# A new slot table for two mixture-of-experts feed-forward layers around a top-k attention, and inputs loaded ahead of weights

## The reference

```python
x = x + 0.5 * ffn(layernorm(x))
x = x + attn(layernorm(x))
x = x + 0.5 * ffn(layernorm(x))
```

## Time and profile before

| | |
|---|---|
| median of 3 runs | 4933.38 us (4929.45 to 4933.44) |
| profiled execution, its own time | 4933.91 us |
| its span | 4932.1 us |
| busy: PE | 4021.6 us (82%) |
| busy: DVE | 4550.9 us (92%) |
| busy: ACT | 3383.9 us (69%) |
| busy: POOL | 3711.1 us (75%) |
| DMA, mean | 47 GB/s |

### The profile page before, as it was taken

The page is one execution under the profiler, slowest core; times in us unless marked ns, Lnnn a source line. Parts: engine busy times, 40 slices in busy tenths (PEclk is TensorE's granted clock), DMA queues, the critical chain, the costliest instruction groups (busy, mean ns, idle before and its releaser), DMA issues.

```text
span 4932.1 us, 111636 instructions
## 1 busy us (share of the span) xinstructions
PE 4021.6 (82%) x29004; PEld 3308.1 (67%) x29004; DVE 4550.9 (92%) x10838; ACT 3383.9 (69%) x8261; POOL 3711.1 (75%) x5070
## 2 busy tenths in 40 slices
PE   5767888888888888888888988888888888877667
PEld 4555766776777667676776767777677677765556
DVE  0199999999999999999999999999999999999990
ACT  2366777777777777777777777777777777766662
POOL 4456788878878787878878787888878788865554
PEclk8887999999999999999999999999999999998778
DMA  2201111111111111111111111111111111111011
GB/s 83 51 20 33 47 50 49 52 48 47 53 46 53 48 51 48 51 50 49 51 46 53 48 50 48 49 51 48 51 48 53 47 52 48 50 38 27 20 28 49
DMA packets 243181, 232.19 MB, mean 47 GB/s; under 512 B 27075, under 2 KB 176580, under 8 KB 242244
## 3 DMA queue, kind: packets, MB, share of 16 engines
q1 hardware_dynamic: 242500, 224.49, 16.5%
HBM read 214.98 MB, written 9.44 MB: 46 GB/s over the span
## 4 chain that ended last, share of the span: by engine, by line
issue 37%; POOL 30%; PE 17%; DVE 10%; ACT 3%; DVEq 1%; POOLq 1%; SPq 1%; ACTq 0%; DMA 0%
POOL HS L899 13%; DVE M L802 6%; PE pQ L490 6%; POOL S L940 6%; POOL mixT L917 4%; DVE W L804 3%; PE pFa L434 2%; PE pFa L438 2%; PE pST L474 1%; PE pST L507 1%; PE pFb L458 1%; PE pFa L378 1%; PE pO L531 1%; DVEq L240 1%; PE pFa L380 1%
## 5 line engine op out<-in xcount | busy, mean ns | idle before, releaser
L490 PE MATMUL pQ<-wf_sb,HS 128*128 128x192 f32 x8192 | 1679.8, 366 | 475.0 <-POOL HS L899 473.7
L802 DVE MAX8 M<-W 128x8 f32<-128x512 f32 x3072 | 1953.4, 675 | 0.0
L490 PEld LDWEIGHTS pQ<-wf_sb,HS 128*128 128x128 f32 x8192 | 1545.1, 216 | 556.5 <-POOL HS L899 431.3
L804 DVE MATCH_REPLACE8 W<-M,W 128x512 f32<-128x512 f32 x2048 | 1363.0, 670 | 0.0
L940 POOL TENSOR_TENSOR S<-S,RL 128x512 f32<-128x512 f32 x1024 | 1306.4, 1277 | 0.0
L706 ACT ACTIVATE RL<-S,NBI 128x512 f32<-128x512 f32 x1024 | 762.4, 745 | 388.9 <-POOL S L940 387.4
L935 POOL TENSOR_TENSOR NBI<-M,edge 128x4 f32<-128x4 f32 x512 | 102.1, 199 | 881.1 <-DVE M L802 850.7
L711 ACT ACTIVATE S<-S,NBI 128x512 f32<-128x512 f32 x1024 | 748.4, 731 | 2.1 <-POOL S L940 2.1
L695 ACT COPY S<-pST 128x512 f32<-128x512 f32 x1024 | 525.2, 600 | 242.7 <-PE pST L474 242.7
L804 DVE MATCH_REPLACE8 W<-M,S 128x512 f32<-128x512 f32 x1024 | 681.5, 670 | 0.0
L802 DVE MAX8 M<-S 128x8 f32<-128x512 f32 x1024 | 648.6, 672 | 29.5 <-issue 28.7
(11 more groups left out here) (219 smaller groups left out, 5477.9 us busy)
## 6 DMA issues: line engine op xcount, KB each, us to landing
RB<-rows_b SPq DMA_DIRECT2D x384, 256.0 KB, 3.2
RB<-rows_a SPq DMA_DIRECT2D x384, 256.0 KB, 3.3
x_b<-in_x SPq DMA_DIRECT2D x64, 128.0 KB, 2.8
out_y<-y SPq DMA_DIRECT2D x64, 128.0 KB, 1.7
wf_sb<-in_wf SPq DMA_DIRECT2D x1, 3072.0 KB, 10.4
wof_sb<-in_wof SPq DMA_DIRECT2D x1, 1024.0 KB, 12.4
rows_b<-rwT_b SPq DMA_DIRECT2D x64, 8.0 KB, 1.3
rows_a<-rwT_a SPq DMA_DIRECT2D x64, 8.0 KB, 1.3
```

Source lines behind the costliest of these rows:

```text
L490: mm = nc.tensor.matmul(pQ[:, 0:QKV], HS[:, k % 2, e, i, :], wf_sb[:, i, at:at + QKV], start=k + e + i == 0, stop=(k, e, i) == (3, 3, 1))
L802: nc.vector.max(m, src[i]).then_inc(s_tk, 1)
L804: nc.vector.match_replace(W[:, i, :], m, src[i], -BIG).then_inc(s_tk, 1)
```

## The change

- All constants of the attention's steps but `TR`, `PTE`, `PV`, `CTT` and `CTX` move. `TOP` goes from even to odd slots.
- Both tables `AT` are new. The gates of job a (`rw_st` to `hs`) are 14 slots ahead of their first use in place of 3, those of job b 11 in place of 4; `rows` is four deep for that. `ctx_rec` of a goes from 37 to 32, `ctx_norm` from 39 to 32, `y` from 87 to 95. In job b, modulo 16, `x_rstd` goes from 3 to 15 and `h` from 4 to 15, `shift` from 8 to 2, `top` from 9 to 2, `repl` from 11 to 3 and `gate` from 14 to 4.
- The projections alternate between the banks of a and b (`PBANK`). The values V0, V1 now come behind the first scores, and the move of V to its place waits for them.
- SP loads all four tiles of x of the first batch, then `wf` in four parts with a semaphore each, then the biases. Everything else of the weights (`late_loads`) comes behind the second `RB` of tile 0.
- The wait for the halved `wof_sb` goes from PE's first chunk to its first `y`; ACT's scaling is in the slot of the first `hs`.

```diff
-SC, EV, TOP, NBIAS, REL, SUB, EXP, TR, PTE, PV, CT, CTT, CTX = 2, 3, 4, 6, 7, 8, 9, 16, 17, 18, 19, 20, 21
+SC, EV, TOP, NBIAS, REL, SUB, EXP, TR, PTE, PV, CT, CTT, CTX = 3, 4, 5, 7, 9, 9, 13, 16, 17, 18, 20, 20, 21
...
 AT = {
-    "a": {k: v - 2 * TILE for k, v in {
-        "ctx_rec": 69, "ctx_norm": 71, "ctxT": 72, "x": 74, "x_mean": 75, "x_sq": 76, "x_rstd": 77, "h": 78,
-        "hT": 79, "h_rinv": 79, "lg": 81, "shift": 82, "top": 83, "pair": 84, "repl": 85, "gate": 87,
-        "gate_exp": 88, "gate_em": 89, "gate_sum": 90, "rw": 91, "rwT": 92, "rw_st": 93, "hs": 96, "qkv": 104,
-        "qkT": 105, "sc": 107, "sc_max": 107, "sc_nmax": 109, "sc_exp": 110, "sc_rec": 111, "sc_norm": 112,
-        "pT": 114, "rb2": 110, "attT": 116, "mix": 117, "y": 119, "out": 120,
-    }.items()},
-    "b": {k: v - SPAN for k, v in {
-        "x_ld": -51, "x_sum": -48, "x_mean": -47, "x_sq": -46, "x_rstd": -45, "h": -44, "hT": -43, "h_rinv": -43,
-        "lg": -41, "shift": -40, "top": -39, "pair": -38, "repl": -37, "gate": -34, "gate_exp": -33,
-        "gate_em": -32, "gate_sum": -31, "rw": -30, "rwT": -29, "rw_st": -28, "hs": -24, "qkv": -16, "qkT": -15,
-        "sc": -14, "sc_max": -13, "sc_nmax": -11, "sc_exp": -10, "sc_rec": -9, "sc_norm": -8, "pT": -6,
-        "rb2": -10, "attT": -4, "mix": -3, "y": 0, "y_mean": 2, "y_sq": 3, "y_rstd": 4, "y_norm": 5, "xn": 8,
+    "a": {
+        "ctx_rec": 32, "ctx_norm": 32, "ctxT": 33, "x": 36, "x_mean": 36, "x_sq": 37, "x_rstd": 37, "h": 39,
+        "hT": 40, "h_rinv": 40, "lg": 41, "shift": 42, "top": 42, "pair": 43, "repl": 44, "gate": 45,
+        "gate_exp": 46, "gate_em": 47, "gate_sum": 49, "rw": 49, "rwT": 50, "rw_st": 50, "hs": 64, "qkv": 72,
+        "qkT": 74, "sc": 75, "sc_max": 76, "sc_nmax": 78, "sc_exp": 79, "sc_rec": 80, "sc_norm": 81, "rb2": 81,
+        "pT": 83, "attT": 85, "mix": 88, "y": 95, "out": 98,
+    },
+    "b": {k: v - 2 * SPAN for k, v in {
+        "x_ld": 10, "x_sum": 10, "x_mean": 12, "x_sq": 14, "x_rstd": 15, "h": 15, "hT": 16, "h_rinv": 16, "lg": 17,
+        "shift": 18, "top": 18, "pair": 19, "repl": 19, "gate": 20, "gate_exp": 21, "gate_em": 23, "gate_sum": 24,
+        "rw": 25, "rwT": 26, "rw_st": 29, "hs": 40, "qkv": 48, "qkT": 50, "sc": 51, "sc_max": 51, "sc_nmax": 53,
+        "sc_exp": 55, "sc_rec": 57, "sc_norm": 57, "rb2": 57, "pT": 59, "attT": 61, "mix": 64, "y": 69,
+        "y_mean": 70, "y_sq": 71, "y_rstd": 71, "y_norm": 75, "xn": 76,
     }.items()},
 }
 
-PROJ = {"Q0": 57 - SPAN, "K0": 59 - SPAN, "V0": 61 - SPAN, "V1": 62 - SPAN, "Q1": 68 - SPAN, "K1": 70 - SPAN}
-VMOVE = 7
+PBANK = {"Q0": "b", "K0": "a", "V0": "b", "V1": "a", "Q1": "b", "K1": "a"}
+PROJ = {"Q0": -2, "K0": 0, "V0": 6, "V1": 7, "Q1": 9, "K1": 6}
+VMOVE = 8
...
 FILLS = {
-    "a": {k: (AT["a"][k], TILE, TILES) for k in ("ctxT", "x", "hT", "lg", "rwT", "qkT", "sc", "pT", "attT", "y")},
+    "a": {k: (AT["a"][k], TILE, TILES) for k in ("ctxT", "x", "hT", "lg", "rwT", "qkT", "sc", "pT", "attT", "y")}
+    | {k: (s, SPAN, NB) for k, s in PROJ.items() if PBANK[k] == "a"},
     "b": {k: (AT["b"][k], TILE, TILES) for k in ("hT", "lg", "rwT", "qkT", "sc", "pT", "attT", "y", "xn")}
-    | {k: (s, SPAN, NB) for k, s in PROJ.items()},
+    | {k: (s, SPAN, NB) for k, s in PROJ.items() if PBANK[k] == "b"},
 }
...
-                self.rows = nc.dram_tensor(f"rows_{n}", (2, E, P), F32, kind="Internal").ap()
+                self.rows = nc.dram_tensor(f"rows_{n}", (TPB, E, P), F32, kind="Internal").ap()
...
-            def early_loads():
-                sp.dma_start(wf_sb[:], wf).then_inc(s_ld_wf, 16)
+            for t in range(TPB):
+                sp.dma_start(b.x[:, t, :], x_t[t]).then_inc(s_ld_x[t], 16)
+            for k in range(4):
+                part = slice(4 * k * QKV, 4 * (k + 1) * QKV)
+                sp.dma_start(wf_sb[:, :, part], wf[:, :, part]).then_inc(s_ld_wf[k], 16)
+            sp.wait_ge(s_ini, 1)
+            for c in range(2):
+                sp.dma_start(bias[:, c, 0, :], bqk[2 * c]).then_inc(s_ld_att, 16)
+                sp.dma_start(bias[HD:P, c, 1, :], bqk[2 * c + 1, 0:P - HD, :]).then_inc(s_ld_att, 16)
+
+            def late_loads():
                 sp.dma_start(wof_sb[:], wof).then_inc(s_ld_wof, 16)
                 for g in range(GROUPS):
...
                     t, c = at
                     if not (isinstance(t, int) and t < TPB):
                         held(sp, q["read"], fill("b", w, j + J.at["y"] - J.at["x_ld"] - SPAN) + 1)
-                    held(sp, q["x_in"], t * 16)
-                    sp.dma_start(J.x[:, c % TPB, :], x_t[ds(t, 1)].rearrange("a p d -> (a p) d")).then_inc(q["x_in"], 16)
-                    if isinstance(t, int) and t == 0:
-                        early_loads()
+                        held(sp, q["x_in"], 16 * t - 16 * TPB)
+                        sp.dma_start(J.x[:, c % TPB, :], x_t[ds(t, 1)].rearrange("a p d -> (a p) d")).then_inc(q["x_in"], 16)
...
                 if at := tile(J, "rw_st", w, j):
                     t, c = at
                     held(sp, q["read"], fill(J.n, w, j + J.at["rwT"] - J.at["rw_st"]) + 1)
-                    if not (isinstance(t, int) and t < 2):
-                        held(sp, s_mix, earlier(w, j + J.at["mix"] - J.at["rw_st"] - 2 * TILE, MIXES.values()) + 1)
-                    sp.dma_start(J.rows[c % 2], J.rwT[:]).then_inc(q["rw_st"], 16)
+                    if not (isinstance(t, int) and t < TPB):
+                        held(sp, s_mix, earlier(w, j + J.at["mix"] - J.at["rw_st"] - SPAN, MIXES.values()) + 1)
+                    sp.dma_start(J.rows[c % TPB], J.rwT[:]).then_inc(q["rw_st"], 16)
                 for k in range(4):
                     if at := tile(J, "hs", w, j, 3 - 2 * k):
                         t, c = at
                         held(sp, q["rw_st"], 16 * t + 16)
                         held(sp, s_hs, chunk_no(w, j + 3) - 1)
                         sp.dma_start(RB[:, k % 2, :, :].rearrange("p e t -> p (e t)"),
-                                     J.rows[c % 2, 4 * k:4 * k + 4, :].rearrange("e t -> (e t)").partition_broadcast(P)
+                                     J.rows[c % TPB, 4 * k:4 * k + 4, :].rearrange("e t -> (e t)").partition_broadcast(P)
                                      ).then_inc(s_rb[k % 2], 16)
+                        if k == 1 and isinstance(t, int) and (J.n, t) == ("b", 0):
+                            late_loads()
...
                 if at := tile(J, "y", w, j, 1):
                     t, c = at
+                    if isinstance(t, int) and (J.n, t) == ("b", 0):
+                        pe.wait_ge(s_half, 1)
...
-                q, F = jobs["b"].sem, jobs["b"].F
                 for c in range(2):
                     for i, key in enumerate((f"Q{c}", f"K{c}")):
                         if not at_proj(key, w, j):
                             continue
-                        wait(pe, q["read"], fill("b", w, j))
+                        J = jobs[PBANK[key]]
+                        wait(pe, J.sem["read"], fill(J.n, w, j))
                         for k in range(KC):
-                            mm = nc.tensor.matmul(F[:], wqk_sb[:, i * KC + k, c * P:(c + 1) * P], xnT[:, k, :],
+                            mm = nc.tensor.matmul(J.F[:], wqk_sb[:, i * KC + k, c * P:(c + 1) * P], xnT[:, k, :],
                                                   start=k == 0, stop=k == KC - 1)
-                        mm.then_inc(q["full"], 1)
+                        mm.then_inc(J.sem["full"], 1)
...
-                        if k == 0 and isinstance(t, int) and t == 0:
-                            pe.wait_ge(s_ld_wf, 16)
-                            pe.wait_ge(s_half, 1)
+                        if isinstance(t, int) and (J.n, t) == ("b", 0):
+                            pe.wait_ge(s_ld_wf[k], 16)
...
-                        key = "K0" if c % QUADS == 0 else "K1"
-                        sl = PROJ[key] - SC - (c % QUADS) * 4 + j
-                        pe.wait_ge(jobs["b"].sem["read"], fill("b", w, sl) + 1)
+                        for key in ("Q0", "K0") if c % QUADS == 0 else ("Q1", "K1"):
+                            J = jobs[PBANK[key]]
+                            sl = PROJ[key] - SC - (c % QUADS) * 4 + j
+                            pe.wait_ge(J.sem["read"], fill(J.n, w, sl) + 1)
...
                 if J.n == "b" and (at := tile(J, "x_sum", w, j)):
                     t, c = at
-                    act.wait_ge(q["x_in"], 16 * t + 16)
+                    if isinstance(t, int) and t < TPB:
+                        act.wait_ge(s_ld_x[t], 16)
+                    else:
+                        act.wait_ge(q["x_in"], 16 * t - 16 * TPB + 16)
...
-                if (w.lo, j) == (FIRST, 20):
+                if (w.lo, j) == divmod(AT["b"]["hs"], SPAN):
...
                     if due(w, j, VMOVE + 4 * g, SPAN, NB):
+                        for key in ("V0", "V1") if g == 0 else ():
+                            J = jobs[PBANK[key]]
```

(34 more changed lines are left out.)

7 lines of the change are left out of this document (4 added, 3 removed).

## The result

The changed kernel takes 5427.29 us (median of four runs, 5411.77 to 5434.53), the kernel before 4932.78: a ratio of 1.0999, 95% interval 1.0985 to 1.1012. It is 10% slower. The prediction said slower with 0.90 and 5292 us in a range of 5115 to 5500, so the sign and the range held and the point lies 135 us too low.

The account below looks back on a forecast made before the run. DVE was taken to bound the middle, which could only grow by its waits. Start 206, middle 4566 plus 404 of waits and end 115 gave a span of 5291, forecast 5292 us, range 5115 to 5500.

Parts of the forecast that it names:

- What bounds: In the middle DVE is busy 4537.3 of 4566 us; it can only get longer, if DVE must wait.
- First wait: DVE at `ctx_rec`, end of block 15, waits for ACT's `ctxr`: 3.1 us in 55 tiles, +171 us.
- upper bound: At `ctx_rec`, a wait of 4.5 us if PE's transposes hold up ACT's copies of PTs.
- Second wait: DVE at `top` of b waits for POOL's `shift`: 4.4 us, 52 times in full, +233 us in all.
- Third place: POOL's `gate` of b waits for `repl`; 23.6 us of work fit 26.2 before `shift` of a: no wait.
- more waits: Rival: DVE waits at `top` of a too, 2 to 4 us in 55 tiles, 5400 to 5510 us; chance 0.10.
- Busy time: DVE's work in the middle: the change takes no instruction from it, so no change was counted.
- Start: Before the first top-k pass: first HS near 30, 3 us a tile for five tiles; 25 us off, to 206.
- End: Behind the last pass: a 6.2 us chain goes for three tiles, about 2 back; 20 us off, to 115.
- Occupancy: Skill's rule to look at the fullest engine; by it DVE alone counts and 4888 us comes out, chance 0.09.

Follow-up runs that it names:

- e1: The changed kernel with `x_sq` and `x_rstd` of job b one slot earlier (13 and 14): 5257.65 us.
- e4: The changed kernel with `mix` of b moved from slot 64 to 66 and `rb2` of a from 81 to 83: 5298.44 us.
- e6: The changed kernel with the subtraction `SUB` alone moved from slot 9 to 10, one behind `REL`: 5364.54 us.
- e3: The changed kernel with `x_sq` and `x_rstd` of b a slot earlier and `ctx_norm` of a a slot later: 5190.92 us.
- e5: The changed kernel with `x_sq` and `x_rstd` of b a slot earlier, `ctx_norm` of a a slot later and `SUB` in slot 10: 4992.09 us.
- e7: The kernel before with `ctx_norm` moved from 71 to 69, the slot of `ctx_rec`: 5058.82 us.
- e12: The changed kernel with `x_sq`, `x_rstd` of b a slot earlier, `ctx_norm` a slot later, `SUB` in 10, ScalarE's copies `CT`, `CTX` at 19, 20: 5173.27 us.
- e8: The kernel before (its table, constants and banks) with the new order of loading and four sets of gate rows: 4929.36 us.
- e2: The changed kernel with `ctx_norm` of a one slot later (32 to 33), behind `ctx_rec`: 5368.95 us.

## Why the prediction was right, and where its sum was off

- **What bounds.** Right: DVE's busy time hardly changed, and the middle grew by what DVE idles.
- **First wait**, +171 predicted: 222.2 us measured, 28.7 of it the loop's turn that is now inside, so +193.5. The mechanism is the one that e1 shows. The size was 3.0 to 3.9 us in a tile against 3.1. Two of the larger ones can be read in ScalarE's timeline: in front of 2192.38 (3.65 us) it copies a part of V as well, and in front of 2272.00 (3.71 us) the last copy of PTs waits 0.27 us for TensorE, the case that the prediction's upper bound had named.
- **Second wait**, +233 predicted: 233.8 measured, from t = 2 (3.94 us; 3.9 predicted) on. e4 shows the price of one item. Counting between two events of the same engine, with nothing assumed of POOL's lag, gave the number.
- **Third place**, 0 predicted in front of `shift` of a, with a margin of 2.6 us; measured 60.7 us, mostly 3.7 in the one tile of four that has projections in slots 6 to 9, and 3.0 in four tiles more. This is the mis-sized term of the middle. I had added POOL's busy times and left out that `SUB` in the slot of `REL` makes POOL wait for ScalarE; e6 takes 56 of the 61 us away with that one slot. The rival "more waits" had named the place, for another reason (y, the norm of x), and put it in 55 tiles; it came in 18. But it was a cause of the same rank as the other two: with their edits made, it held 199 us, as e3 against e5 shows. Leaving it out cost the sum only 61 us because the first two waits covered most of it. The prediction had not counted on that, and to that extent its closeness is luck.
- **Busy time**, 0 predicted, +25 measured. A small operation that follows a block directly can add nothing (in the changed kernel the block in front of `v_a` at 2075.58 ends at 2075.66, and the next block starts there). One that is waited for stands alone: 0.22 us from `v_b` at 2040.18 to the next M, and the same from `crec` at 2026.75. At 127 waits the 25 us are 0.2 us each, an estimate from the two totals.
- **Start**, -25 predicted, -6.4 measured: the step that failed. The first HS came at 28.93 us (30 predicted, 37.26 in the earlier trace rows), 8.3 us earlier, which the new order of loading explains. The 15 us counted on top, 3 in each of five tiles for gates ahead, did not come. POOL's waits between 60 and 200 us, four tiles, the kernel before first and the one after below:

```profile
POOL rgs_b L889 <- ACT eg_b L572: 20.5, 4, 7.3
```

```profile
POOL mny L941 <- ACT x1r L671: 20.9, 4, 6.2
```

The wait for the gate's exponential went, and with it the wait for RB, which was only 8.5 us in these four tiles. In the same tiles a wait for `x1r`, the end of y, came, of 20.9 us: POOL works 76.1 of these 140 us before and 78.1 after. b's y now stands between two tiles' HS on POOL. I had named that and still counted a gain. That y is what took it back is read from these waits, not tested.
- **End**, 115 predicted, 117 measured. The size is right; the reason given, the gates' chain of 6.2 us in three tiles, isn't borne out. POOL's waits for RB behind the last pass fell only from 7.3 to 4.2 us. Its busy time there fell from 66.8 to 61.5 us, and the rest is in other waits. No run takes this apart.
- **Occupancy.** The Trainium skill (Perfetto Trace Analysis, "Identifying the Most-Contended Engine") points to the engine of the highest occupancy. The trace agrees on the engine, 92% before and 84% after, and that figure says nothing of the 517 us: they came from engines at 69% (POOL) and 62% (ACT).

So of the 135 us, 22 are the first wait, 1 the second, 61 the third place, 25 the busy time, 18 the start (223.6 against 206), 2 the end, together 129; 3 are the median's distance from the profiled span (4.3 against the 1.3 assumed), 1 is where the middle was cut, and 2 are DVE's short gaps.

## What to carry to other kernels

In a statically ordered pipeline, write for each small operation of the bound engine which gap between its long blocks it falls into, and count time in blocks, not in slots: between two gaps the other engine must do all of its queued work, of any job. A result used in the same gap or slot in which another engine makes it is a lock, and two engines that each wait for the other's latest result hold each other in the same way. Undo such locks together before judging one, since each hides a part of the others (e3, e5). One alone can cost 2.6%, with a wait that shows at a third engine (e7). Work moved ahead of a wait pays only if nothing takes its place between the same two steps.

## What the runs showed of the hardware

TensorE's mean granted clock over the run was 0.915 before and 0.877 in the changed kernel. It doesn't tell the time: e3 and e5 both have 0.893, at 5191 and 4992 us, and e12 has 0.903 at 5163. Its matmul of HS took 377 ns on average between 1000 and 4000 us, 362 in the kernel before (granted clock 0.89 and 0.94 there).

The busy time of DVE for the same 10838 instructions rose with the number of waits for small operations in the middle: 4550.9 us with none in the kernel before, 4551.2 with none in e8, 4560.3 with 41 in e5, 4561.9 with 58 in e7, 4575.7 with 127 in the changed kernel and 4582.9 with 161 in e2.
